# Four passes of a two-layer transformer kernel: loops on the engines against passes written out

## The reference, cut to what matters

```python
x = x + attn(layernorm(x), W_qkv_a, b_qkv_a, W_out_a, b_out_a)    # x: (2, 1024, 512), 16 heads of 32, causal
x = x + ffn(layernorm(x), w_gate, w_up, w_down)                   # 512 -> 2048 -> 512, silu(gate) * up
x = x + attn(layernorm(x), w_qkv_b, b_qkv_b, w_proj_b, b_proj_b)
x = x + ffn(layernorm(x), w_gate, w_up, w_down)                   # the same weights
```

## Time and profile before

| | |
|---|---|
| three runs | 2031.79, 2034.46, 2035.56 us, median 2034.46 |
| the profiled execution | 2035.76 us |
| its span, from the first to the last instruction | 2034.0 us |
| mean granted clock of TensorE | 0.997 |
| TensorE's matmuls | 1982.6 us, 97% of the span |
| VectorE, GpSimd, ScalarE | 57%, 49%, 40% |
| transfers | 134 MB, mean 66 GB/s |

### The profile page before, as it was taken

One profiled execution on the slowest core, in us unless ns is written; L12 is line 12 of the kernel. 1 busy time (PEld: TensorE's weight loads), 2 busy tenths in 40 slices (PEclk: granted clock), 3 DMA queues, 4 the chain that ended last, 5 costly groups with the idle time before them and its releaser, 6 DMA issues.

```text
span 2034.0 us, 34492 instructions
## 1 busy us (share of the span) xinstructions
PE 1982.6 (97%) x10304; PEld 1442.5 (71%) x10304; DVE 1168.1 (57%) x2404; ACT 813.8 (40%) x1481; POOL 999.4 (49%) x775
## 2 busy tenths in 40 slices
PE   7999999999999999999999999999999999999998
PEld 5555588888755558888765555888887555688887
DVE  4767555445577755454457775545456767544454
ACT  2388522221158742222115874222221676432221
POOL 4224359753312437975331243797533223389743
PEclk9999999999999999999999999999999999999999
DMA  4333111111333310111243331111113333111112
GB/s 150 90 79 90 33 42 54 51 63 42 85 75 85 74 43 32 62 53 52 73 136 75 85 75 43 32 63 52 52 43 85 74 84 75 43 42 63 53 53 83
DMA packets 59177, 134.07 MB, mean 66 GB/s; under 512 B 10720, under 2 KB 11744, under 8 KB 58976
## 3 DMA queue, kind: packets, MB, share of 16 engines
q1 hardware_dynamic: 58976, 131.66, 23.0%
HBM read 76.57 MB, written 4.19 MB: 40 GB/s over the span
## 4 chain that ended last, share of the span: by engine, by line
PE 89%; issue 3%; ACT 3%; DVE 2%; DMA 2%; POOL 0%; SPq 0%; DVEq 0%; ACTq 0%; POOLq 0%
PE bank L1306 11%; PE bank L1308 11%; PE bank L1307 11%; PE bank L1442 10%; PE ring L1306 10%; PE ring L1307 10%; PE ring L1308 10%; PE bank L1415 8%; PE ring L1384 7%; PE ring L1297 1%; ACT masked L831 1%; DMA area<-nm_lo 1%; ACT prob L809 1%; DMA x<-x_in 1%; DVE xn L1039 0%
## 5 line engine op out<-in xcount | busy, mean ns | idle before, releaser
L809 ACT ACTIVATE prob<-bank 128x512 f32<-128x512 f32 (+1 forms) x512 | 271.9, 571 | 143.5 <-PE bank L1415 115.1
L611 POOL TENSOR_SCALAR area<-w_stage 128x1024 fp32r<-128x1024 f32 x129 | 139.5, 1082 | 366.8 <-PE bank L1308 206.3
L688 POOL TENSOR_SCALAR_AFFINE_SELECT prob<-prob 128x512 f32<-128x512 f32 x128 | 82.9, 648 | 479.5 <-ACT prob L809 339.8
L613 POOL TENSOR_TENSOR area<-w_stage,area 128x1024 fp32r<-128x1024 f32 x129 | 309.2, 2397 | 10.8
L1110 DVE TENSOR_TENSOR x<-x,bank 128x512 f32<-128x512 f32 x256 | 171.1, 685 | 234.3 <-PE bank L1308 233.1
L1039 DVE CUSTOM_DVE_ANT_0 xn<-ring,mask_row 128x384 bf16<-128x384 f32 (+7 forms) x384 | 246.3, 661 | 86.7 <-PE ring L1384 84.4
L1306 PE MATMUL ring<-xt_hi,area 128*128 128x512 f32 x672 | 266.3, 396 | 1.6 <-DVE area L1143 1.0
L1307 PE MATMUL ring<-xt_lo,area 128*128 128x512 f32 x672 | 262.9, 391 | 0.0
L1308 PE MATMUL ring<-xt_hi,area 128*128 128x512 f32 x672 | 262.6, 391 | 0.0
L1415 PE MATMUL bank<-area 98*128 98x512 f32 (+3 forms) x768 | 247.8, 380 | 7.1 <-DMA area<-nm_lo 3.9
L1384 PE MATMUL ring<-area 96*128 96x512 f32 (+3 forms) x768 | 227.4, 362 | 9.9 <-DVE row_max L1039 5.5
(11 more groups left out here) (166 smaller groups left out, 3626.5 us busy)
## 6 DMA issues: line engine op xcount, KB each, us to landing
w_stage<-ffn_w SPq DMA_DIRECT2D x96, 512.0 KB, 3.3
area<-kq_parts SPq DMA_DIRECT2D x336, 128.0 KB, 2.3
w_stage<-attn_w SPq DMA_DIRECT2D x35, 512.0 KB, 3.3
area<-attn SPq DMA_DIRECT2D x48, 128.0 KB, 2.3
x<-x_in SPq DMA_DIRECT2D x20, 256.0 KB, 3.9
out<-x SPq DMA_DIRECT2D x16, 256.0 KB, 2.5
bias_rows<-row_bias SPq DMA_DIRECT2D x10, 256.0 KB, 4.4
area<-nm_hi SPq DMA_DIRECT2D x32, 8.0 KB, 1.8
```

The source lines that it names most:

```text
L611: pool.tensor_scalar(hi, src, 1.0, 0.0, ALU.mult, ALU.add).then_inc(w_hi_done, 1)
L613: pool.tensor_tensor(lo, src, hi.bitcast(F32), ALU.subtract).then_inc(w_split, 1)
L809: act.activation(prob[:, step % PROB_BUFS, h, off:], scores_at(u, j, h), ACT.Exp, scale=SCALE).then_inc(prob_ready, 1)
```

## The change

The four passes are written out by Python. `it`, `b` and `layer` become integers on every engine, so each wait has a constant; and with that `wait_alone` goes: each of its calls is a plain `wait_ge` for the one semaphore, which the compiler can put into the operation behind it. Where two waits stand ahead of one operation, as in `maximum` for units 3 and 5, one of them stays an instruction. The order of operations, transfers, tiles and semaphores is the same on every engine.

```diff
-        def wait_alone(eng, semaphore, value):
-            if not isinstance(value, int):
-                value = eng.snap(eng.to_reg(value))
-            eng.wait_ge(const_ready, CONSTS)
-            eng.wait_ge(semaphore, value)
...
@@ sync
                 if i >= 2 or it is not None:
-                    wait_alone(sp, w_split, (0 if it is None else it * SLOTS) + i - 1)
+                    sp.wait_ge(w_split, (0 if it is None else it * SLOTS) + i - 1)
...
             def stack_max(it, u):
-                wait_alone(sp, ring_drained, drained(it, ("mt", u)))
+                sp.wait_ge(ring_drained, drained(it, ("mt", u)))
...
             for b in range(BATCH):
-                with sp.Fori(0, LAYERS) as layer:
+                for layer in range(0, LAYERS):
...
-                            wait_alone(sp, rows_drained, rows_taken(b * LAYERS + LAYERS, t - TT))
+                            sp.wait_ge(rows_drained, rows_taken(b * LAYERS + LAYERS, t - TT))
...
-                            wait_alone(sp, x_stored[t], b * 16 + 16)
+                            sp.wait_ge(x_stored[t], b * 16 + 16)
...
@@ gpsimd
-                        wait_alone(pool, product_full, products(it, *after[1:]))
+                        pool.wait_ge(product_full, products(it, *after[1:]))
...
-                wait_alone(pool, prob_ready, it * S2_STEPS + GH * (step + 1))
+                pool.wait_ge(prob_ready, it * S2_STEPS + GH * (step + 1))
...
-            with pool.Fori(0, BATCH * LAYERS) as it:
+            for it in range(0, BATCH * LAYERS):
...
@@ scalar
-            with act.Fori(0, BATCH * LAYERS) as it:
+            for it in range(0, BATCH * LAYERS):
...
@@ vector
-                wait_alone(dve, stats_done, 2 * n - CT)
+                dve.wait_ge(stats_done, 2 * n - CT)
...
-                    wait_alone(dve, ring_full, full(it, name))
+                    dve.wait_ge(ring_full, full(it, name))
                     if u in SUMMED:
                         k = tile_index(u, s)
-                        wait_alone(dve, row_summed, it * SUM_TILES + k + 1)
+                        dve.wait_ge(row_summed, it * SUM_TILES + k + 1)
...
-            with dve.Fori(0, BATCH) as b:
-                with dve.Fori(0, LAYERS) as layer:
+            for b in range(0, BATCH):
+                for layer in range(0, LAYERS):
...
@@ tensor
-            with pe.Fori(0, BATCH * LAYERS) as it:
+            for it in range(0, BATCH * LAYERS):
```

More of the change, by code:

```diff
@@ L509, in stack_qk @@
                 if u in SIDE_UNITS:
-                    wait_alone(sp, side_taken, side_done(it, ("k", u)))
+                    sp.wait_ge(side_taken, side_done(it, ("k", u)))
                 else:
-                    wait_alone(sp, ring_drained, drained(it, ("k", u)))
+                    sp.wait_ge(ring_drained, drained(it, ("k", u)))
                 kb, qb = k_buffer(u), K_BUFS + q_buffer(u)
@@ L554, in _ @@
                     load_weights(11, it, own)
-                    wait_alone(sp, out_bias_added, it * TT + TT)
+                    sp.wait_ge(out_bias_added, it * TT + TT)
                     load_biases(1 - layer)
@@ L585, in split_weights @@
                 n = it * SLOTS + i
-                wait_alone(pool, w_loaded[j % 2], (it * (SLOTS // 2) + i // 2 + 1) * 16)
+                pool.wait_ge(w_loaded[j % 2], (it * (SLOTS // 2) + i // 2 + 1) * 16)
                 b, part = divmod(j - FFN_SLOT0, 3)
@@ L631, in quad_sums @@
                 pool.tensor_tensor(s3, a11, a21, ALU.subtract).then_inc(s_step, 1)
-                wait_alone(pool, s_step, s_steps(it, b, w, 0))
+                pool.wait_ge(s_step, s_steps(it, b, w, 0))
                 pool.tensor_tensor(s2, s1, a11, ALU.subtract).then_inc(s_step, 1)
-                wait_alone(pool, s_step, s_steps(it, b, w, 2))
+                pool.wait_ge(s_step, s_steps(it, b, w, 2))
                 pool.tensor_tensor(s4, a12, s2, ALU.subtract).then_inc(s_step, 1)
@@ L659, in diff_sum @@
                 if step:
-                    wait_alone(pool, diff_step, it * 6 + step)
+                    pool.wait_ge(diff_step, it * 6 + step)
                 pool.tensor_tensor(dst, a, b, op).then_inc(diff_step, 1)
@@ L694, in split_attn @@
                 cols = slice(c * CHUNK, (c + 1) * CHUNK)
-                wait_alone(pool, side_full, side_done(it, ("k", UNITS - 1)))
-                wait_alone(pool, attn_ready, it * UNITS + u + 1)
+                pool.wait_ge(side_full, side_done(it, ("k", UNITS - 1)))
+                pool.wait_ge(attn_ready, it * UNITS + u + 1)
                 pool.tensor_scalar(xt_hi[:, g, cols], attn[:, g, cols], 1.0, 0.0, ALU.mult, ALU.add
@@ L715, in _ @@
             inverse_deviation(0, 0, 0)
-            wait_alone(pool, xn_ready, CT)
+            pool.wait_ge(xn_ready, CT)
             for i in V_SLOTS:
                 hi, lo = w_part(i, slice(0, SLOT))
-                wait_alone(pool, w_hi_done, i + 1)
+                pool.wait_ge(w_hi_done, i + 1)
                 pool.tensor_tensor(lo, w_stage[:, i, :], hi.bitcast(F32), ALU.subtract).then_inc(w_split, 1)
@@ L730, in _ @@
                     pool.tensor_tensor(x[:, t, :], x[:, t, :], bias_rows[:, 1, :], ALU.add).then_inc(out_bias_added, 1)
-                wait_alone(pool, out_bias_added, it * TT + TT)
+                pool.wait_ge(out_bias_added, it * TT + TT)
                 pool.memset(k_stack[3 * HEAD:3 * HEAD + 2, 0, :, :].bitcast(F32), 1.0).then_inc(ones_ready, 1)
@@ L750, in _ @@
                 inverse_deviation(it, 1, 1)
-                wait_alone(pool, xn_ready, it * 2 * TT + 2 * TT)
+                pool.wait_ge(xn_ready, it * 2 * TT + 2 * TT)
                 for i in range(FFN_SLOT0 + 3, SLOTS + 2):
                     if i == DIFFS_AT:
-                        wait_alone(pool, ring_drained, drained(it, ("ln2", 3)))
+                        pool.wait_ge(ring_drained, drained(it, ("ln2", 3)))
                         for n in range(6):
@@ L758, in _ @@
                     split_weights(it, i)
-                wait_alone(pool, product_full, products(it, QUAD_LAST, "m3", 1))
-                wait_alone(pool, w_split, it * SLOTS + SLOTS + 2)
+                pool.wait_ge(product_full, products(it, QUAD_LAST, "m3", 1))
+                pool.wait_ge(w_split, it * SLOTS + SLOTS + 2)
                 pool.memset(k_stack[3 * HEAD:3 * HEAD + 2, 1:, :, :].bitcast(F32), 1.0).then_inc(ones_ready, 1)
-                wait_alone(pool, ones_ready, 2 * it + 3)
+                pool.wait_ge(ones_ready, 2 * it + 3)
                 inverse_deviation(it + 1, 0, 0)
```

18 lines of the change are left out of this document (9 added, 9 removed).

## The result

| | before | after |
|---|---|---|
| median of the runs (lowest to highest) | 2034.07 us (2031.79 to 2036.66), 6 runs | 2023.98 us (2019.94 to 2025.37), 6 runs |
| profiled execution, its span | 2035.76, 2034.0 | 2023.91, 2021.9 |
| instructions in the span | 34492 | 28276 |

The ratio is 0.9948, 95% interval 0.9935 to 0.996: 10.1 us by the medians (8 to 13 by the interval), against 7.4 forecast. The changed kernel timed again (e10) gave 0.9952 (0.9938 to 0.9965). So the sign and, roughly, the size were right. The sum hides that one term was right, one too small by a factor of three, that two shares were not foreseen at all, and that ScalarE lost by the change.

A forecast was written before the change was run, and what follows sets the result against it. TensorE, busy 97% of the span, was taken to bound the kernel, leaving its idle time and handoffs between engines. Terms of 5 + 0.4 + 1.0 + 0.7 + 0.3 = 7.4 us gave 2027 us, range 2021 to 2031 (8 in 10: 2013 to 2037).

The forecast's parts named there:

- Term 1: VectorE's row maxima in the attention: awaited ones start 0.10 us earlier; 5 us gain, between 2.8 and 11.
- Term 2: SyncE's passing on of the row of maxima and the exchange of x: transfers issued earlier, 0.4 us gain.
- Term 3: ScalarE's and GpSimd's waits before the last values: register steps go, waits stay; 1.0 us gain, between 0 and 1.8.
- Term 4: TensorE's branch at the end of each pass: nearly hidden, 0.7 us gain from what shows at two borders.
- The rest of the pass the same: Outside the four attention phases, each shorter by 1 to 2 us, a pass keeps its time.
- What adds: Costs of the change: no engine instruction added, order kept, and fetching the four times longer program keeps up.
- (c): Rival, slower: small transfers before attention units land later beside weight transfers started earlier; 2039 us at 1.7 us more each; chance 0.13.
- (a): Rival, nothing to measure: register steps run beside work and ScalarE's handoff takes VectorE's place; 2033.8 us; chance 0.2 with (d).
- (d): Rival: compiler keeps separate waits before the maxima, only register steps and branches go, about 2 us; chance 0.2 with (a).
- (b): Rival, much faster: TensorE's own register steps pace the short matmuls of L1442; 16 us more, 2011 us; chance 0.12.
- The clock: Granted clock's fall to 0.52 for 7 us after the exchange of x: stays, nothing counted; 3.4 us possible.
- The sum: All terms for the whole kernel: 7.4 us gain, between about 0 and 18; median 2027 us.

The follow-up runs named there:

- e10: The changed kernel timed again, unchanged: 2024.31 us, ratio 0.9952.
- e2: The changed kernel with only the waits of VectorE's maxima (ring_full, row_summed) standing alone again: 2026.65 us, ratio 0.9954.
- e7: The kernel before with only VectorE's loops written out and only its maxima's waits put at the operation: 2029.03 us, ratio 0.9967.
- e3: The changed kernel with only GpSimd's 25 edited waits standing alone again: 2025.43 us, ratio 0.9944.
- e8: The kernel before with only GpSimd's loop written out and its waits put at the operation: 2030.18 us, ratio 0.9973.
- e11: The changed kernel with ScalarE's wait for the scores put ahead of its wait for free probabilities at a step's first exponential: 2018.55 us, ratio 0.9921.
- e4: The kernel before with only TensorE's loop written out: 2032.54 us, ratio 0.9983.
- e9: The changed kernel with TensorE's loop put back and nothing else: 2027.54 us, ratio 0.9962.
- e6: The changed kernel with 128 more instructions (satisfied waits) at TensorE's start: 2031.18 us, ratio 0.9978.
- e1: The changed kernel, still written out, with the 36 edited waits each standing alone again behind a wait on a constant: 2030.27 us, ratio 0.9969.
- e12: The changed kernel with TensorE's later-fulfilled wait put first at transposes of maxima, masked values and a head's first scores: 2020.15 us, ratio 0.993.
- e5: The changed kernel with 64 more instructions (satisfied waits) at TensorE's start: 2027.7 us, ratio 0.996.

## Why the prediction was right, and where it wasn't

**Term 1, the maxima: right.** 5 us forecast, between 2.8 and 11. Taken away alone they cost 4.6 us (e2), added alone they give 4.9 (e7), nearly all in the attention, whose four phases gained 1.4, 2.4, 1.9 and 0.9 us where 1 to 2 each was forecast. The steps under it hold too: separate wait 0.13 us, attached 0.02, and TensorE's waits for maxima 5.5 to 3.2 us.

**Term 2, SyncE: not separated.** No run put SyncE's waits back by themselves. The issue of the row of maxima does start earlier, 0.03 us behind the end of L1064 in place of 0.08, in the median of 32: the 0.05 of the forecast's upper value.

**Term 3, ScalarE and GpSimd before the last values: right for GpSimd, wrong in sign for ScalarE.** GpSimd's waits take 1.2 us of the attention when put back (e3), and e8 fits 1.0. For ScalarE I wrote "Register steps go, waits stay" and took 0.15 us each time. The waits did not stay where they were: with the register steps went the place that carried the early wait, the wait for the scores became separate, and an awaited exponential starts 0.06 us later. By e11 that costs some 2.5 us, where I had forecast a gain.

**Term 4, the branches: the mechanism was right, the size was not.** 0.7 us forecast; at 518, 1021 and 1527 us the changed kernel gained 0.8, 0.8 and 0.5 us, 2.2 in all, and TensorE's loop alone is worth 3.1 (e4) and 2.7 (e9) on the borders (this includes the stall near 1012 us, where the changed kernel gains 0.6 us). Two steps of it failed. I wrote "At 1020 it shows too, but TensorE then waits for x in any case" and counted nothing; the wait for x comes 14 us later, its release moved too, and the matmul behind it starts 7.3 us earlier than before (1036.82, now 1029.50), where the one at 1021 us starts 7.5 us earlier. So nearly all of it was kept. And I held that L1003 keeps TensorE 0.05 us at 517, and took the chain's 0.57 for the whole; from start to start the gap was 0.96 us there, and it is now as short as any between two matmuls:

```profile
515.08 0.39 PE L1300 MATMUL bank<-area 128*128 128x512 f32 x1
515.31 0.39 PE L1298 MATMUL ring<-area,xt_hi 128*128 128x512 f32 x1
515.53 0.39 PE L1299 MATMUL ring<-area,xt_hi 128*128 128x512 f32 x1
```

**"The rest of the pass the same": wrong, 3.3 us.** The gain of the feed-forward part is one stall in each pass. VectorE's subtraction of diff_lo takes 1.2 us when nothing is beside it (the minimum in before and e3). Before, in pass 0, from the timeline (start us, us, engine, line):

```profile
323.05 2.40 POOL L613 TENSOR_TENSOR area<-w_stage,area 128x1024 fp32r<-128x1024 f32 x1
...
323.50 3.04 DVE L1117 TENSOR_TENSOR diff_lo<-attn,diff_hi 128x1024 fp32r<-128x1024 f32 x1
...
325.41 2.03 POOL L611 TENSOR_SCALAR area<-w_stage 128x1024 fp32r<-128x1024 f32 x1
...
326.46 2.47 DVE L1110 TENSOR_TENSOR x<-x,bank 128x512 f32<-128x512 f32 x4
...
327.19 0.50 PE L1306 MATMUL bank<-xt_hi,area 128*128 128x512 f32 x1 [0.89 <-DVE x L1110]
```

After:

```profile
320.94 2.40 POOL L605 TENSOR_TENSOR area<-w_stage,area 128x1024 fp32r<-128x1024 f32 x1
...
322.34 2.07 DVE L1109 TENSOR_TENSOR diff_lo<-attn,diff_hi 128x1024 fp32r<-128x1024 f32 x1
...
323.30 2.02 POOL L603 TENSOR_SCALAR area<-w_stage 128x1024 fp32r<-128x1024 f32 x1
...
324.34 2.47 DVE L1102 TENSOR_TENSOR x<-x,bank 128x512 f32<-128x512 f32 x4
```

Read the ends. Before, GpSimd's subtraction ends at 325.45 and VectorE's 1.09 us later, at 326.54; after, at 323.34 and 324.41, again 1.07 later. VectorE does its 1.2 us of work behind GpSimd's operation, and GpSimd's next one (2.03 us where 1.06 is its usual time) waits for VectorE in turn. The Trainium skill (SBUF — State Buffer, Who interferes with whom) says that a VectorE instruction with two inputs in SBUF contends with a GpSimd instruction that reads SBUF. The trace agrees, with 3.04 us for 1.2. GpSimd ends 2.1 us earlier, 1.2 of which the whole kernel is earlier at this place; 0.9 us come from the sums and the split ahead of it, each of which has a wait, some on GpSimd's own previous result, that no longer stands alone. The two engines do not meet less often than before: VectorE's 16 subtractions take 2.45 us in the median now and 1.45 before, and the one at 316.90 us takes 3.04 in place of 1.63. They meet where TensorE isn't waiting. Then add_rows (L1102) starts 2.1 us earlier too, and TensorE, which waits for it, loses 0.8 us less in this pass. e3 shows it by putting GpSimd's waits back alone:

```profile
323.79 2.75 DVE L1114 TENSOR_TENSOR diff_lo<-attn,diff_hi 128x1024 fp32r<-128x1024 f32 x1
326.46 2.47 DVE L1107 TENSOR_TENSOR x<-x,bank 128x512 f32<-128x512 f32 x4
```

The add starts at 326.46 again, and TensorE's matmul behind it at 327.28. The stall was in the profile of before, with add_rows as its releaser. I passed over it because the window said 99%; 1% of 1000 us was the size of the whole forecast.

**"What adds": wrong in kind.** "No engine instruction is added" was wrong: the register steps went, but ScalarE got 728 separate waits more and TensorE 624. And I argued that a fault of fetching would show as gaps in the feed-forward part, and held fetching for harmless. No such gap shows, but where a fetch stands beside the 8 KB that TensorE waits for, these land later. Before, 10 of 32 transfers of nm_lo were late, 6.5 us over 1.42 each in sum, of which TensorE idled 3.9; after 1.8 and 1.3. Written-out code happened to gain by this, and e6, with 128 instructions more, has 10 late ones again and 2.5 us idle. These are rival (c)'s landings with the other sign, and with fetches beside them where (c) had weight transfers first of all.

**The rivals.** (a) fell: it had 0.7 us, measured were 10.1. Its remark that ScalarE's waits "already stand at the operation" was true of the kernel before only. (d) fell at the maxima, by the profile after; on ScalarE the compiler did what (d) feared. (b), TensorE's own register steps as pace, fell in e4: its gain in the attention lies at the landings of nm_lo, not along the matmuls of L1442; outside the landings its attention lost 1.1 us.

**The clock.** It still fell behind the exchange of x, for 6.8 us as before; in other executions it fell for 3.4 us or not at all, as in e3. The two profiled executions of the changed kernel differ by 2.7 us, 2.1 of them from 1028 to 1046 us. For the other runs, which have no profile, it is not shown.

**The sum.** By the profiles the change gives 12.8 us outside the half-speed stretches, by the medians 10.1, with an interval that ends at 13. On the borders and in the feed-forward part the shares close: 2.7 to 3.1 us from TensorE's loop against 2.9, and 2.7 to 3.7 from GpSimd's waits against 3.3. In the attention the gains add up to more than the whole: 4.6 to 4.9 us from the maxima, 2.6 from the landings (idle time for nm_lo 3.9 to 1.3) and 1.0 to 1.2 from GpSimd, against 6.6. What the list lacks is the loss on ScalarE, some 2.5 us by e11. With it the sum is 5.7 to 6.2, and e1's is 2.2 less 2.5, about nothing, against 0.8 measured. So it closes within about 1 us; it is an estimate from differences of single profiles. Some is given back as well where ScalarE's row sums set the pace: at the transpose of unit 5's maxima TensorE's gap grew in every pass, from 0.42 to 0.46 us up to 1.11 to 1.14. That nothing else overlaps is not shown.

## What to carry to other kernels

Where a wait stands costs more than that it is there: put the one that is fulfilled last first, so that it sits in the operation, above all where another engine waits for that operation in turn. Look at this on every engine after a change of the loops, also on those whose waits were not edited: here the change gained on three engines and lost on a fourth, and a swap of two waits there took some 2.5 us back. Where two versions of a kernel issue the same matmuls, compare their starts one by one before reading any sum; two profiles of one kernel agreed to 0.2 us in each kind of stretch, where single runs of it lie up to 5 us apart. And an engine at 99% of a long stretch may still hold the stall that you look for: list its idle gaps there, not the share.

## What was not expected of the hardware

- A separate wait that is already fulfilled costs TensorE 0.11 us of its queue (13.8 us for 128, e6).
- A piece of TensorE's instruction stream (16 KB) beside an 8 KB transfer makes this take 2.01 us in the mean in place of 1.42 (84 against 364 transfers).
- An operation that VectorE or ScalarE sits waiting for starts 0.02 us behind its release when it carries the wait. When the wait is an instruction of its own, it is 0.13 us on VectorE (the maxima) and 0.08 on ScalarE (the exponentials).
- TensorE's first large matmuls start every 0.43 us in some executions and every 0.23 in others; from 16 to 20 us this costs 1.6 to 2.1 us (e1 to e4, e8 and e12, not before, after, e5 to e7 and e9 to e11). The views print a granted clock of 1.00 there, but the first record of the granted clock begins only at 19.9 to 21.4 us in these six, within 0.2 us of where the spacing changes. So they show nothing of the clock in that stretch.
